# A graph layer with residual and layer norm: the middle loads three to a ring slot, the last group in a slot of its own, its last k-tiles as weights, and w needed later

## The reference

```python
def reference(x, adj, w, W_agg):
    agg = adj @ (x @ W_agg)                       # [8192, 8192] @ [8192, 64]
    y = x + w[:, None] * relu(agg) + (1.0 - w)[:, None] * x
    m, v = mean(y, axis=-1), var(y, axis=-1)
    return (y - m) / sqrt(v + 1e-5)
```

## Time and profile before

| | us |
|---|---|
| median of three executions | 647.93 |
| the profiled execution, its own time | 651.25 |
| span of the trace | 649.4 |
| PE busy | 520.8 (80%) |
| VectorE busy | 51.0 (8%) |
| ScalarE busy | 13.4 (2%) |
| share of the chain of waits that is DMA | 72% |
| bytes read from HBM | 270.60 MB |

### The profile page before, as it was taken

How to read it: one execution, slowest core, us unless ns; L and a number is a source line. 1 busy time by engine, 2 the same in 40 slices (tenths; PEclk the granted TensorE clock), 3 DMA queues, 4 the chain that set the end, 5 groups by cost and what they waited for, 6 DMA issues and landing times.

```text
span 649.4 us, 7590 instructions
## 1 busy us (share of the span) xinstructions
PE 520.8 (80%) x3526; PEld 270.5 (42%) x3526; DVE 51.0 (8%) x87; ACT 13.4 (2%) x25; POOL 0.7 (0%) x7
## 2 busy tenths in 40 slices
PE   1699999877768868769869777968778887877986
PEld 1575554434334434334434333434334433433435
DVE  0140000300000300000300000300000300000302
ACT  1110000000000000000000000000000000000000
POOL 0000000000000000000000000000000000000000
PEclk9999999979899988898897798988898889988999
DMA  9999999999999999999999999999999999999796
GB/s 374 443 417 392 432 420 435 444 424 442 426 424 444 431 437 429 419 444 437 426 437 424 437 439 429 424 439 429 444 429 419 444 424 444 431 421 425 286 407 234
DMA packets 11256, 272.82 MB, mean 420 GB/s; under 512 B 1648, under 2 KB 2288, under 8 KB 3952
## 3 DMA queue, kind: packets, MB, share of 16 engines
q1 hardware_dynamic: 9792, 270.54, 97.2%
q10 hardware_dynamic: 1456, 2.16, 0.9%
HBM read 270.60 MB, written 2.10 MB: 420 GB/s over the span
## 4 chain that ended last, share of the span: by engine, by line
DMA 72%; PE 26%; SPq 1%; DVE 0%; issue 0%; ACT 0%; ACTq 0%; DVEq 0%
DMA ring<-adj_main_dram 65%; PE bank L183 22%; DMA w_sb<-w_dram 4%; DMA ring<-adj_last_dram 2%; PE bank L172 2%; DMA ring<-adj_mid_dram 1%; PE bank L209 1%; PE bank L156 1%; SPq L137 1%; DVE xw L289 0%; ACTq L240 0%; PE bank L192 0%; ACT aggT L261 0%; SPq L123 0%; PE bank L218 0%
## 5 line engine op out<-in xcount | busy, mean ns | idle before, releaser
L183 PE MATMUL bank<-ring,xw 128*64 128x320 f32 x3072 | 462.5, 464 | 94.7 <-DMA ring<-adj_main_dram 93.7
L183 PEld LDWEIGHTS bank<-ring,xw 128*64 128x64 f32 x3072 | 230.4, 147 | 324.8 <-DMA ring<-adj_main_dram 115.1
L313 DVE TENSOR_TENSOR y<-bank,w_sb 128x320 f32<-128x320 f32 x12 | 5.3, 487 | 528.1 <-PE bank L192 528.1
L209 PE MATMUL bank<-ring,xw 128*64 128x384 f32 x128 | 21.4, 489 | 2.5 <-DMA ring<-adj_mid_dram 2.5
L172 PE MATMUL bank<-wagg,xT 64*128 64x64 f32 x128 | 15.5, 423 | 6.4 <-DVE xw L289 6.4
L156 PE MATMUL bank<-ident,xres 128*128 128x128 f32 x32 | 8.9, 431 | 13.8 <-DMA xres<-x_dram 9.0
L172 PEld LDWEIGHTS bank<-wagg,xT 64*128 64x128 f32 x128 | 14.2, 325 | 8.8 <-issue 8.8
L261 ACT ACTIVATE aggT<-bank 128x640 f32<-128x640 f32 x6 | 4.2, 704 | 531.7 <-PE bank L183 531.7
L209 PEld LDWEIGHTS bank<-ring,xw 128*64 128x64 f32 x128 | 9.0, 137 | 14.5 <-issue 9.6
L156 PEld LDWEIGHTS bank<-ident,xres 128*128 128x128 f32 x32 | 5.7, 216 | 14.9 <-issue 9.0
L218 PE MATMUL bank<-ring,xw 128*64 128x128 f32 x128 | 7.6, 275 | 1.5 <-DMA ring<-adj_last_dram 1.5
(11 more groups left out here) (27 smaller groups left out, 15.9 us busy)
## 6 DMA issues: line engine op xcount, KB each, us to landing
ring<-adj_main_dram SPq DMA_DIRECT2D x48, 5120.0 KB, 38.6
ring<-adj_mid_dram SPq DMA_DIRECT2D x7, 1536.0 KB, 10.5
xres<-x_dram SPq DMA_DIRECT2D x1, 2048.0 KB, 8.1
out_dram<-xres ACTq DMA_DIRECT2D x6, 320.0 KB, 16.7
ring<-adj_last_dram SPq DMA_DIRECT2D x1, 1024.0 KB, 7.3
ring<-adj_mid_dram SPq DMA_DIRECT2D x1, 960.0 KB, 10.3
ring<-adj_last_dram SPq DMA_DIRECT2D x1, 832.0 KB, 9.0
ring<-adj_last_dram SPq DMA_DIRECT2D x1, 640.0 KB, 10.1
```

The source lines that it names most:

```text
L183: last = nc.tensor.matmul(acc[h * D:(h + 1) * D, b, 0:CHUNK], xw[:, j], ring[:, slot, at:at + CHUNK], start=j == 0, stop=j == T - 1)
L209: last = nc.tensor.matmul(mid_acc[h * D:(h + 1) * D, b, 0:MID_CHUNK], xw[:, j + s], ring[:, load % RING, at:at + MID_CHUNK], start=j + s < ...
```

## The change

1. w is loaded by SP's queue right behind x, and no longer by ScalarE's queue. On VectorE the wait for w and the step that makes 2 - w stand behind the xw copies.
2. The last main group is written out behind the loop of the other five, on SP and on PE. Its last load (number 47) is issued as four loads of 2 k-tiles each (`MAIN_TAIL`), with a semaphore for each.
3. The mid group is eight loads of 8 k-tiles. Three of them lie side by side in one ring slot: 0 to 2 in slot 0, 3 to 5 in slot 1, 6 and 7 in slot 2. Each has a semaphore of its own, and the queue waits only at loads 0, 3 and 6, for the contraction of main loads 44, 45 and 46.
4. The last group's ten loads go to slot 3 and wait for the contraction of main load 47.
5. The turn back of the last main group stands on PE behind the first mid load's matmuls.
6. The last three loads of the last group (2 k-tiles each) are contracted the other way round: the adjacency tile (128 columns) is the stationary operand and xw streams, so that the result is already in rows. It is accumulated in `last_rows`, a PSUM bank of its own, and the turned-back sum of the first 58 k-tiles is added there by one matmul just ahead of the last two k-tiles.

```diff
-MID_LOADS = (8, 8, 8, 8, 8, 8, 8, 5, 3)
+MAIN_TAIL = (2, 2, 2, 2)
+MID_RUN = 3
 LAST_LOADS = (16, 13, 10, 7, 5, 4, 3, 2, 2, 2)
+DIRECT_LOADS = 3
...
             sp.dma_start(xres[:], x.rearrange("(p t) d -> p t d", p=P)).then_inc(x_in, 16)
+            sp.dma_start(w_sb[:], w.rearrange("(p t) -> p t", p=P)).then_inc(w_in, 16)
...
-            with sp.Fori(1, G) as g:
+            with sp.Fori(1, G - 1) as g:
...
-            for i, n in enumerate(MID_LOADS):
-                load = MID_LOAD0 + i
-                sp.wait_ge(slot_free, load - RING + 1)
-                sp.dma_start(ring[:, load % RING, 0:n * MID_SLOTS * P],
...
-            sp.wait_ge(slot_free, LAST_LOAD0 - RING + 1)
+            for c in range(C - 1):
+                sp.wait_ge(slot_free, (G - 1) * C + c - RING + 1)
+                sp.dma_start(ring[:, c % RING], adj_main[G - 1, c].rearrange("q s n -> q (s n)")).then_inc(loaded[c % RING], 16)
+            sp.wait_ge(slot_free, G * C - RING)
+            s = 0
+            for k, n in enumerate(MAIN_TAIL):
+                sp.dma_start(ring[:, RING - 1, s * COLS:(s + n) * COLS],
+                             adj_main[G - 1, C - 1, :, s:s + n].rearrange("q s n -> q (s n)")).then_inc(main_tail_loaded[k], 16)
+                s += n
+            for c in range(C):
+                if c % MID_RUN == 0:
+                    sp.wait_ge(slot_free, G * C + c // MID_RUN - RING + 1)
+                at = c % MID_RUN * SUB * MID_SLOTS * P
+                sp.dma_start(ring[:, c // MID_RUN, at:at + SUB * MID_SLOTS * P],
+                             adj_mid[c].rearrange("q s n -> q (s n)")).then_inc(mid_loaded[c], 16)
+            sp.wait_ge(slot_free, G * C)
             j = 0
             for k, n in enumerate(LAST_LOADS):
-                sp.dma_start(ring[:, LAST_LOAD0 % RING, j * P:(j + n) * P],
+                sp.dma_start(ring[:, RING - 1, j * P:(j + n) * P],
...
-            with pe.Fori(0, G) as g:
+            with pe.Fori(0, G - 1) as g:
...
+            for c in range(C - 1):
+                pe.wait_ge(loaded[c % RING], arrivals((G - 1) * C + c))
+                contract(c % RING, c * SUB, 0, SUB).then_inc(slot_free, 1)
...
+            for k, n in enumerate(LAST_LOADS[-DIRECT_LOADS:]):
+                pe.wait_ge(last_loaded[len(LAST_LOADS) - DIRECT_LOADS + k], 16)
+                if k == DIRECT_LOADS - 1:
+                    pe.wait_ge(agg_copied, LAST + 1)
+                    nc.tensor.matmul(last_rows, aggT[:, 0:P], ident2[:], start=False, stop=False)
+                for s in range(n):
+                    last = nc.tensor.matmul(last_rows, ring[:, RING - 1, (j + s) * P:(j + s + 1) * P], xw[:, j + s],
+                                            start=j + s == DIRECT_J0, stop=j + s == T - 1)
+                j += n
+            last.then_inc(rows_done, 1)
...
-            act.dma_start(w_sb[:], w.rearrange("(p t) -> p t", p=P)).then_inc(w_in, 16)
...
-            act.wait_ge(slot_free, LAST_LOAD0)
+            act.wait_ge(mid_done, 1)
...
-            dve.wait_ge(w_in, 16)
-            step(nc.vector.tensor_scalar(two_minus_w[:], w_sb[:], -1.0, 2.0, ALU.mult, ALU.add), 1)
             for b in range(BLOCKS):
...
+            dve.wait_ge(w_in, 16)
+            step(nc.vector.tensor_scalar(two_minus_w[:], w_sb[:], -1.0, 2.0, ALU.mult, ALU.add), 1)
...
-            step(nc.vector.tensor_scalar(v, rows_ps[:, 0:D], 0.0, w_sb[:, t:t + 1], ALU.max, ALU.mult), LAST_STEP0 + 1)
+            step(nc.vector.tensor_scalar(v, last_rows, 0.0, w_sb[:, t:t + 1], ALU.max, ALU.mult), LAST_STEP0 + 1)
```

More of the change, by code:

```diff
@@ L41, in gnn_residual_layernorm @@
     BLOCKS = T // 2 // PB
-    MID_LOAD0 = G * C
-    LAST_LOAD0 = MID_LOAD0 + len(MID_LOADS)
-    assert C * SUB == T == sum(MID_LOADS) == sum(LAST_LOADS) and LAST_T0 + LAST_SLOTS == T and C % RING == 0
+    MID_SLOT_LOADS = -(-C // MID_RUN)
+    DIRECT_J0 = T - sum(LAST_LOADS[-DIRECT_LOADS:])
+    assert C * SUB == T == sum(LAST_LOADS) and LAST_T0 + LAST_SLOTS == T and C % RING == 0
+    assert sum(MAIN_TAIL) == SUB and MID_RUN * MID_SLOTS <= MAIN_SLOTS and MID_SLOT_LOADS < RING
     DVE_PRE = 2
@@ L92, in gnn_residual_layernorm @@
         last_acc = bank[:, 0]
+        last_rows = bank[:, 1, 0:D]
         rows_ps = bank[:, 6:8].rearrange("p b n -> p (b n)")
         loaded = [sem(f"loaded{r}") for r in range(RING)]
+        main_tail_loaded = [sem(f"main_tail_loaded{k}") for k in range(len(MAIN_TAIL))]
+        mid_loaded = [sem(f"mid_loaded{c}") for c in range(C)]
         last_loaded = [sem(f"last_loaded{k}") for k in range(len(LAST_LOADS))]
@@ L102, in gnn_residual_layernorm @@
         xw_done, xw_copied = sem("xw_done"), sem("xw_copied")
-        last_done = sem("last_done")
+        mid_done, last_done = sem("mid_done"), sem("last_done")
         agg_copied = sem("agg_copied")
@@ L124, in _ @@
                                  adj_main[bass.ds(g, 1), c].rearrange("o q s n -> (o q) (s n)")).then_inc(loaded[c % RING], 16)
-            j = 0
-            for i, n in enumerate(MID_LOADS):
-                load = MID_LOAD0 + i
-                sp.wait_ge(slot_free, load - RING + 1)
-                sp.dma_start(ring[:, load % RING, 0:n * MID_SLOTS * P],
-                             adj_mid[j // SUB, :, j % SUB:j % SUB + n].rearrange("q s n -> q (s n)")
-                             ).then_inc(loaded[load % RING], 16)
-                j += n
-            sp.wait_ge(slot_free, LAST_LOAD0 - RING + 1)
+            for c in range(C - 1):
[14 more added lines that the diff above has]
+            sp.wait_ge(slot_free, G * C)
             j = 0
             for k, n in enumerate(LAST_LOADS):
-                sp.dma_start(ring[:, LAST_LOAD0 % RING, j * P:(j + n) * P],
+                sp.dma_start(ring[:, RING - 1, j * P:(j + n) * P],
                              adj_last[:, j:j + n].rearrange("q s n -> q (s n)")).then_inc(last_loaded[k], 16)
@@ L175, in _, with contract @@
             pe.wait_ge(xw_copied, BLOCKS)
-            def contract(slot, j0):
-                for s in range(SUB):
+            def contract(slot, j0, s0, n):
+                for s in range(s0, s0 + n):
                     j = j0 + s
@@ L184, in contract @@
                                                     start=j == 0, stop=j == T - 1)
-                last.then_inc(slot_free, 1)
+                return last
             def turn_back(g):
@@ L193, in turn_back @@
                 last.then_inc(rows_done, 1)
-            with pe.Fori(0, G) as g:
+            with pe.Fori(0, G - 1) as g:
                 for c in range(C):
                     pe.wait_ge(loaded[c % RING], g * (16 * C // RING) + arrivals(c))
-                    contract(c % RING, c * SUB)
+                    contract(c % RING, c * SUB, 0, SUB).then_inc(slot_free, 1)
                 turn_back(g)
-            j = 0
[L202 to L214, removed]
+            for c in range(C - 1):
+                pe.wait_ge(loaded[c % RING], arrivals((G - 1) * C + c))
+                contract(c % RING, c * SUB, 0, SUB).then_inc(slot_free, 1)
+            s = 0
+            for k, n in enumerate(MAIN_TAIL):
+                pe.wait_ge(main_tail_loaded[k], 16)
+                last = contract(RING - 1, T - SUB, s, n)
+                s += n
+            last.then_inc(slot_free, 1)
+            for c in range(C):
+                pe.wait_ge(mid_loaded[c], 16)
+                for s in range(SUB):
+                    j = c * SUB + s
+                    h = j % 2
+                    for b in range(MID_BANKS):
+                        at = (c % MID_RUN * SUB + s) * MID_SLOTS * P + b * MID_CHUNK
+                        last = nc.tensor.matmul(mid_acc[h * D:(h + 1) * D, b, 0:MID_CHUNK], xw[:, j],
+                                                ring[:, c // MID_RUN, at:at + MID_CHUNK], start=j < 2, stop=j >= T - 2)
+                if c == 0:
+                    turn_back(G - 1)
+            last.then_inc(mid_done, 1)
+            j = 0
+            for k, n in enumerate(LAST_LOADS[:-DIRECT_LOADS]):
                 pe.wait_ge(last_loaded[k], 16)
@@ L218, in _ @@
                     last = nc.tensor.matmul(last_acc[h * D:(h + 1) * D, 0:P], xw[:, j + s],
-                                            ring[:, LAST_LOAD0 % RING, (j + s) * P:(j + s + 1) * P],
-                                            start=j + s < 2, stop=j + s >= T - 2)
+                                            ring[:, RING - 1, (j + s) * P:(j + s + 1) * P],
+                                            start=j + s < 2, stop=j + s >= DIRECT_J0 - 2)
                 j += n
@@ L231, in _ @@
             last.then_inc(last_done, 1)
-            pe.wait_ge(agg_copied, LAST + 1)
-            pe.wait_ge(dve_step, MID * DVE_GROUP + DVE_PRE + 1)
-            nc.tensor.matmul(rows_ps[:, 0:D], aggT[:, 0:P], ident2[:], start=True, stop=True).then_inc(rows_done, 1)
+            for k, n in enumerate(LAST_LOADS[-DIRECT_LOADS:]):
[8 more added lines that the diff above has]
```

(1 more changed line is left out.)

## The result

The changed kernel takes 645.38 us (median of seven executions, 645.12 to 645.56). Beside it the kernel before took 649.37 us (646.57 to 652.26). The ratio is 0.9939, with a 95% interval of 0.9913 to 0.9964: faster by 4.0 us, 0.6%. The forecast was 641.0, and its range ended at 645, so the time lies above it. The profiled execution of the changed kernel has a span of 643.3 us and a time of its own of 645.12, so between the two profiled executions the gain is 6.1 us, where 7.0 were forecast; between the medians it is 4.0. These are two different misses. Of the 4.4 us between 641.0 and 645.38, 0.8 is the first (a time of its own of 645.12 for 644.3), 3.3 is what the forecast took off to get from the profiled execution to the median, and 0.3 is what the changed kernel's median lies above its profiled execution.

The account below looks back on a forecast made before the run. The DMA engines' pace bounds the main part; time is won only where they idle and behind the last byte. Start 1.4 plus 606 us hole and rest 5.6 make 7.0 us, off the median 640.9; predicted 641.0, range 638 to 645.

Parts of the forecast that it names:

- The two holes: Stretches at 56 us and 606 to 611 us where the DMA engines run dry; the change was to close both.
- the transfer to the median: Final step: the 7.0 us gain taken off the median, 3.3 us below the profiled execution, giving 640.9 us.
- the row of 11.76 us: PE's contraction of main load 47 from 597.48 us, at 0.66 of its clock, for 8.84 us normally.
- The start: Moving the wait for w behind the xw copies closes the hole at 56 us: 1.4 us gained.
- The landings from load 47 on: Mid loads queue behind main load 47 without a gap; the last mid load lands at 626.4 us.
- the first rival: Late DMA engines, from program fetches, or one slow clock spell move the end 0.6 to 2 us: 642 to 644; chance 0.22.
- The 0.2 us for load 47 in four pieces: Cost taken for shorter rows when main load 47 is split; bounds 0 and 0.6 us.
- The end: PE's chain from the last mid landing at 626.4 us until VectorE starts at 638.5; PE the bound by about 0.3 us.
- the direct k-tiles: Last group's six k-tiles with adjacency stationary: 0.27 us each taken, bounds 0.114 and 0.43; four of them 1.1 us.
- the queue never ran thin: Rival before the last group: SP's issues held up, half of the 4 us at 606 stays, 643 to 645; chance 0.08.
- The price of about 2 us for each load: Rival at load 47: three additional pieces each stop the queue, 6 us, 647 us, no change; chance 0.03.
- TensorE's clock: Rival in the mid stage: PE drops to its lower clock after pauses, mid loads take 5.4 us, 664 us; chance 0.04.

Follow-up runs that it names:

- experiment 4: The kernel before with only the ring slots changed (mid loads three to a slot, last group in slot 3): 644.59 us, ratio 0.9915.
- the execution of 647.30: A further profiled execution of the kernel before, nothing changed: 647.30 us, where the median of its twelve executions was 648.73.
- Experiment 5: The changed kernel with the last main group in the loop and load 47 whole: 643.84 us; with only load 47 whole: 645.27; unchanged: 645.34.
- set B: Runs on one chip of the changed kernel and variants with load 47 whole or the loop kept, beside the kernel before at 648.78 us.

## Why the prediction was right and wrong

**The two holes** were read rightly, as was what closes them. The share is full at 56 and at 609 us, all mid loads follow main load 47 without a gap, and experiment 4 shows that the gain is where the slots were changed.

**The step that failed** is the transfer to the median: "The median of the runs shown is 3.3 us below the profiled execution; the same 7.0 off it gives 640.9". The profiled execution was slow because both its holes were long. The second misses 4.0 us of share, where the execution of 647.30 misses 1.4, through a contraction that began at the lower clock; the first cost it 1.4 us more. Closing a hole gives the median only the hole of a median execution. So the 7.0 us belong off 651.25, which gives 644.3 for a profiled execution that took 645.12, and not off the median. That the profiled time lay 3.3 us above the median, and that three executions spread over 3.3 us, were the signs. The forecast itself had the row of 11.76 us beside those of 8.84, and used it only as a danger for the new kernel. The changed kernel is on the other side of this: none of its executions is more than 0.4 us from the median, since it has no such wait left, and the median lies 0.3 above the profiled execution. Three executions were also few: the median of seven was 649.37, that of three 647.93.

**The start**, 1.4 us, was of the right size for the profiled execution: main load 46 is contracted from 583.72 on instead of 585.36, 1.6 earlier. In the mean of five traces it is 1.1 us at load 47. Alone it gave 0.2 in the median, not to be told from nothing, with the second hole still there, and about 0.9 with the new slots. The working had the order of events right but not their cause in full: PE's work on main load 0 began at 33.4 us and not at 39.1, because the second load of W_agg, issued by the same queue as w, lands after 7.8 us and not 13.6, so that the second block's transposes no longer wait.

**The landings from load 47 on** came 1.1 us late (627.5 for 626.4). All of it is there at load 47's last piece, which landed at 597.26, where the sum had 596.0; from there to the last mid landing it is 30.3 us, 30.4 in the sum. This is the first rival, which had a chance of 0.22. Experiment 5 puts 1.5 us on it, inside the 0.6 to 2 that the rival gave. Its cause, the longer program of PE, was named there too, as about four more fetches. But its price was from two or three fetches on one engine at 0.6 us each, an estimate by bytes; the traces have 1.09 us for the fetch, and one did it. The 0.2 us for load 47 in four pieces had no row behind it; the runs have 0.07, which is nothing that can be told.

**The end.** The chain behind the last mid landing was forecast at 12.1 us and took 11.8; the direct k-tiles take 1.10/4 = 0.275 us each, 0.27 was taken from line 228. That PE and not the last load is the bound was right, and with it that the direct form gives back what the copy and turn back had cost.

**The other rivals** did not come true. SP's issues were held up, up to 7.0 us for one of the last loads, but the queue never ran thin. The price of about 2 us for each load, from the Trainium skill, "DMA: Bandwidth & Descriptors", section "Anatomy of one DMA — SWDGE (gpsimd) path", does not show in a full queue: load 47 in four pieces and in one take 645.34 and 645.27 us. The prediction also read its row for this price wrongly: most of the two empty us at 608 to 610 lie before mid load 3 is issued at 609.3, and its first packets move at 610.2, 0.9 us later. TensorE's clock stayed at 1.00 from 605 to 640 us, where PE stopped for 0.6 to 1.4 us at a time. The argument against this rival was thinner than it looked, since it had four rows: in the same trace, loads at 243.66 and 316.41 us took 10.52 us after idle times of 2.10 and 1.65.

Together: slots 4.0, w 0.2 to 0.9, direct k-tiles 0, pieces of load 47 0, the written-out group 1.5 lost. That is 2.7 to 3.4 us, where the whole measured 3.4 beside the kernel before in set B and 4.0 in the first result; the intervals of the single steps are about as wide as what is left over.

## What to carry to other kernels

A profile is one execution. Before a stall in it is counted as gain, look at what sets its length: if it ends with work whose duration has more than one value in the same trace, the gain is an average over them, and the spread of the timed runs tells how far apart they are. Take the forecast gain off the execution in which it was read, not off the median. In a kernel bound by its loads, a hole in the DMA queue is also the place where late engines catch up: in the trace of the kernel before, the sixteen arrivals of mid load 2 lie 2.0 us apart, and those of mid load 3, behind the hole, 0.5. When the holes are closed, whatever burdens the latest engine, such as a longer program, can go straight to the end.

## What the runs showed of the hardware that was not expected

- Fetches of program take the same DMA engines as the data: 16 KB in 0.9 to 1.1 us as one packet, four for a written-out group of 256 fp32 matmul calls (512 matmuls and 512 weight loads in the trace), none in the passes of a loop after the first one (no fetch between 105 and 613 us with the loop kept). One of the four met a queue that never empties where it widened the distance between the first and the last engine by 1.2 to 1.4 us, in each of three traces, and there it stayed; the other three left the landings where they were.
- A small load in the queue of another engine was slow beside large ones: w, 32 KB, landed after 25.2 us from ScalarE's queue, and after 8.1 from SP's, ahead of the ring loads. Its neighbour, the second load of W_agg, went from 13.6 to 7.8 us by its going (7.7 with w alone moved).
- With ten loads under way, SP's issue of a single one took up to 7.0 us instead of 0.33 to 0.43.
